# Re-ordering the openings of two deformable-convolution layers: group 0's hats and first dense rows go ahead of bilinear weights, second tap and image 1's sums

## The reference, cut to what matters

```python
off1 = make_offset(conv3x3(x, tm1_w, tm1_b), conv3x3(x, tr1_w, tr1_b))
out = deform_conv(x, off1, dcn1_w)
out = jax.nn.relu(batchnorm(out, bn1_g, bn1_b))
off2 = make_offset(conv3x3(out, tm2_w, tm2_b), conv3x3(out, tr2_w, tr2_b))
out = deform_conv(out, off2, dcn2_w)
out = batchnorm(out, bn2_g, bn2_b)
return jax.nn.relu(out + residual)

# deform_conv: for each pixel and each of 9 taps, 4 corners of x at a
# fractional position, weighed bilinearly; then a product over channels and taps
cols = corner(y0i, x0i, (1 - wy) * (1 - wx)) + corner(y0i, x0i + 1, (1 - wy) * wx) \
     + corner(y0i + 1, x0i, wy * (1 - wx)) + corner(y0i + 1, x0i + 1, wy * wx)
return jnp.einsum('nckhw,ock->nohw', cols, w.reshape(Co, C, K))
```

## Time and profile before

| | us |
|---|---|
| median of 3 runs | 776.32 |
| lowest, highest | 775.11, 782.59 |
| the profiled execution | 783.84 |
| its span, first to last instruction | 782.0 |

### The profile page before, as it was taken

How to read it: one execution, slowest core, us unless ns; L and a number is a source line. 1 busy time by engine, 2 the same in 40 slices (tenths; PEclk the granted TensorE clock), 3 DMA queues, 4 the chain that set the end, 5 groups by cost and what they waited for, 6 DMA issues and landing times.

```text
span 782.0 us, 12373 instructions
## 1 busy us (share of the span) xinstructions
PE 738.1 (94%) x3497; PEld 457.3 (58%) x3497; DVE 598.9 (77%) x1605; ACT 509.3 (65%) x1269; POOL 461.6 (59%) x458
## 2 busy tenths in 40 slices
PE   7889999999999999968999999989998999899997
PEld 6646656555555554654666555545554544678786
DVE  5498879798888879359887998868886878767542
ACT  1756766777777776447776777767776856664342
POOL 3777767777777776067777787777777740000000
PEclk8689999999999999857999999999999999999999
DMA  6969765665766777166886556666777720000001
GB/s 204 312 184 275 244 184 162 195 196 180 207 197 204 207 209 201 55 209 194 246 262 197 174 167 189 182 205 191 207 208 211 208 79 1 1 1 28 1 28 55
DMA packets 55103, 130.13 MB, mean 166 GB/s; under 512 B 8271, under 2 KB 24944, under 8 KB 55036
## 3 DMA queue, kind: packets, MB, share of 16 engines
q0 software_dynamic: 35200, 115.37, 49.4%
q1 hardware_dynamic: 19820, 13.94, 5.7%
q10 hardware_dynamic: 16, 0.03, 0.0%
HBM read 118.76 MB, written 10.55 MB: 165 GB/s over the span
## 4 chain that ended last, share of the span: by engine, by line
PE 76%; DVE 10%; DMA 5%; ACT 4%; issue 3%; POOL 1%; SPq 0%; DVEq 0%; POOLq 0%; ACTq 0%
PE pair L1338 26%; PE pair L1353 10%; PE bank L1497 5%; PE bank L1287 5%; DMA G<-table,rowi 5%; PE bank L1289 4%; PE pair L1322 4%; PE pair L1345 3%; PE pair L1457 2%; PE pair L1432 2%; PE bank L1322 2%; PE pair L1304 2%; PE pair L1479 2%; PE pair L1152 2%; DVE U L928 2%
## 5 line engine op out<-in xcount | busy, mean ns | idle before, releaser
L542 POOL DMA_INDIRECT G<-table,rowi x440 | 453.6, 1031 | 174.0 <-issue 93.9
L1338 PE MATMUL pair<-ST,XT 128*128 128x512 f32 x544 | 261.6, 613 | 7.7 <-ACT CTD L661 7.7
L624 ACT ACTIVATE V<-G,wgt 128x128 f32<-128x128 f32 x440 | 175.1, 398 | 39.1 <-DMA G<-table,rowi 38.4
L626 ACT ACTIVATE U<-G,wgt 128x128 f32<-128x128 f32 x440 | 171.6, 390 | 0.0
L1338 PEld LDWEIGHTS pair<-ST,XT 128*128 128x128 f32 x544 | 105.6, 196 | 109.9 <-issue 83.5
L928 DVE SCALAR_TENSOR_TENSOR V<-G,wgt,V 128x128 f32<-128x128 f32 x440 | 152.5, 347 | 3.7 <-ACT U L626 3.6
L978 DVE TENSOR_TENSOR ST<-pair,stacks 128x512 f32<-128x512 f32 x180 | 119.0, 685 | 45.3 <-PE pair L1322 29.4
L928 DVE SCALAR_TENSOR_TENSOR U<-G,wgt,U 128x128 f32<-128x128 f32 x440 | 152.7, 347 | 0.0
L691 ACT COPY CT<-bank 128x512 f32<-128x512 f32 x110 | 64.3, 585 | 79.2 <-PE bank L1289 70.0
L1353 PE MATMUL pair<-CT,dcn_T 128*128 128x512 f32 x220 | 112.2, 593 | 0.0
L1287 PE MATMUL bank<-band,V 128*128 128x128 f32 x440 | 99.4, 276 | 0.0
(11 more groups left out here) (173 smaller groups left out, 757.3 us busy)
## 6 DMA issues: line engine op xcount, KB each, us to landing
table<-XT SPq DMA_DIRECT2D x16, 512.0 KB, 5.2
G<-table,rowi POOLq DMA_INDIRECT x440, 3.7
out_dram<-G SPq DMA_DIRECT2D x8, 256.0 KB, 2.0
X<-in_x_dram SPq DMA_DIRECT2D x3, 512.0 KB, 6.7
A<-in_L_conv_dcn_w_dram SPq DMA_DIRECT2D x2, 576.0 KB, 8.4
X<-in_x_dram SPq DMA_DIRECT2D x2, 256.0 KB, 2.8
table<-zeros SPq DMA_DIRECT2D x4, 16.0 KB, 2.0
qkv_nat<-in_L_conv_wv_dram SPq DMA_DIRECT2D x1, 64.0 KB
```

What stands on the lines that cost most here:

```text
L542: pool.indirect_dma_start(G[:, i % UNITS, r, :], None, table(n).rearrange("r (e k) -> r e k", e=2), bass.IndirectOffsetOnAxis(rowi[:, at:a ...
L624: act.activation(V[:, i % V_RING, r, :], G[:, i % UNITS, r, 0:C], ACT.Copy, scale=wgt[:, tile:tile + 1, 0])
L626: act.activation(U[:, i % V_RING, r, :], G[:, i % UNITS, r, 3 * C:4 * C], ACT.Copy, scale=wgt[:, tile:tile + 1, 3]).then_inc(scaled[l], 1)
L1338: last = pe.matmul(dense_acc, XT[:, g // IGROUPS * TS + t, :], ST[:, all_y % ST_RING, :], start=(t == 0), stop=(t == QT - 1))
```

## The change

Only order changes, with one bank of accumulators and two row counts. No operation is added or taken away.

- **ROWS.** Group 0's dense rows are used 3, 3, 2 a tap (was 2, 3, 3 and 3, 3, 2).
- **DVE.** `bilinear_weights(0)` is cut in three and interleaved with the hats of group 0, which now start first; `xt_copy(1)` goes behind both. The products of step 0's rows go ahead of `corner_sums(0)` and `offsets(1)`. Positions and row numbers of image 1 go from ahead of the main loop to the end of step 1.
- **PE.** `sum_x(1)` and `sum_y(1)` go between the steps of tap 0's hats; the first three rows are spread ahead of `sum_y(1)`, the second tap and the three setups; `turn(0)` goes behind step 0's dense rows.
- **ACT.** `hats_middle(0)` and `hats_copy(0, 0)` go ahead, and the scalings of blocks 0 and 1 are cut in halves between the copies.
- **PSUM.** Image 1's products go to `conv_acc`, so that `turn_hats(0, 0)` no longer waits for image 1's `z_copy`.

```diff
-        ROWS = [[2, 3, 3, 3, 3, 2], SLOW, QUICK, ...]
+        ROWS = [QUICK, SLOW, QUICK, ...]
@@
-            return (hat_acc if n < AHEAD else job_acc)[:, 0:TS * TAPS * NOFF]
+            return (hat_acc, conv_acc, job_acc)[min(n, AHEAD)][:, 0:TS * TAPS * NOFF]
@@ ACT
                 hats_top(0)
+                hats_middle(0)
                 z_copy(1)
-                hats_middle(0)
+                hats_copy(0, 0)
+                act.wait_ge(wgt_ready, l * N + 1)
+                scale(0, range(0, GTILES // 2))
                 u_copy(1)
-                act.wait_ge(wgt_ready, l * N + 1)
-                scale(0, range(GTILES))
-                hats_copy(0, 0)
+                column_copy(0, 0)
+                scale(0, range(GTILES // 2, GTILES))
                 if l == 0:
                     setup(1)
-                column_copy(0, 0)
+                hats_copy(0, 1)
                 if l == 0:
                     setup(2)
-                hats_copy(0, 1)
+                scale(1, range(0, GTILES // 2))
+                column_copy(0, 1)
                 if l == 0:
                     setup(3)
-                column_copy(0, 1)
-                scale(1, range(GTILES))
+                scale(1, range(GTILES // 2, GTILES))
                 scale(2, range(GTILES))
@@ DVE
-                bilinear_weights(0)
-                xt_copy(1)
@@
                 hats_first(0)
+                corner_distances(0)
                 hats_split(0)
+                corner_hats()
                 hats_last(0)
+                corner_products(0)
+                xt_copy(1)
+                for now in USED[0]:
+                    product(*now)
                 dve.wait_ge(wgt_ready, l * N + 1)
                 corner_sums(0)
                 offsets(1)
-                for now in USED[0]:
-                    product(*now)
                 corner_sums(1)
                 add_halves(1)
                 hats_first(1)
-                dve.wait_ge(off_ready, l * N + AHEAD)
-                positions(1, AHEAD)
-                sample_rows(1, AHEAD)
@@ DVE, end of step i
+                    if i == POSITIONS_NEXT:
+                        dve.wait_ge(off_ready, l * N + AHEAD)
+                        positions(1, AHEAD)
+                        sample_rows(1, AHEAD)
@@ PE
                     products(n, 1)
-                    sum_x(n)
-                    sum_y(n)
+                    if n == 0:
+                        sum_x(n)
+                        sum_y(n)
@@
                 turn_hats(0, 0)
-                if l == 0:
-                    setup(1)
+                sum_x(1)
                 spread_columns(0, 0)
-                if l == 0:
-                    setup(2)
-                turn_hats(0, 1)
-                if l == 0:
-                    setup(3)
-                spread_columns(0, 1)
-                turn(0)
                 pe.wait_ge(xt_dve, l * N + AHEAD)
                 pe.wait_ge(xt_act, l * N + AHEAD)
                 for now in USED[0]:
                     spread_rows(*now)
+                sum_y(1)
+                if l == 0:
+                    setup(1)
+                turn_hats(0, 1)
+                if l == 0:
+                    setup(2)
+                spread_columns(0, 1)
+                if l == 0:
+                    setup(3)
                 for now in USED[1]:
                     spread_rows(*now)
@@ PE, main loop, behind use_dense
+                    if i == 0:
+                        turn(0)
```

More of the change, by code:

```diff
@@ L283, in deform_resblock_attention @@
         RELU = {at - 2: n for n, at in TURN_AT.items()}
+        POSITIONS_NEXT = 1
         POSITIONS = max(SUM_Y) + 1
@@ L291, in deform_resblock_attention @@
         SLOW, QUICK = [2, 2, 2, 2, 3, 3, 2], [3, 3, 2, 3, 3, 2]
-        ROWS = [[2, 3, 3, 3, 3, 2], SLOW, QUICK, QUICK, QUICK, [3, 3, 2] * DENSE[5], SLOW, QUICK]
+        ROWS = [QUICK, SLOW, QUICK, QUICK, QUICK, [3, 3, 2] * DENSE[5], SLOW, QUICK]
         BEGIN = [FIRST[g] - (g > 0) for g in range(GROUPS)]
@@ L876, in sample_rows, with corner_distances @@
                 step(dve.tensor_scalar(low[:, 1, tiles], low[:, 1, tiles], ROUND + W - 2, -ROUND, ALU.min, ALU.add))
-            def bilinear_weights(n):
+            def corner_distances(n):
                 tiles = tile_range(n, n + 1)
@@ L883, in bilinear_weights, with corner_hats @@
                 step(dve.tensor_scalar(dist[:, 1], dist[:, 0], -1.0, None, ALU.add))
+            def corner_hats():
                 for e in range(2):
@@ L889, in bilinear_weights, with corner_products @@
                 step(last)
+            def corner_products(n):
+                tiles = tile_range(n, n + 1)
                 for s, (dy, dx) in enumerate(CORNERS):
@@ L892, in bilinear_weights @@
                 last.then_inc(wgt_ready, 1)
+            def bilinear_weights(n):
+                corner_distances(n)
+                corner_hats()
+                corner_products(n)
             for l in range(LAYERS):
@@ L1299, in turn_hats @@
                     else:
-                        pe.wait_ge(z_act, l * N + AHEAD)
+                        pe.wait_ge(z_act, l * N + 1)
                     to = hat_acc.bitcast(bf16)[0:HK, :].rearrange("q (a t p) -> q a t p", a=2, t=GTILES)
```

## The result

The changed kernel takes 774.75 us (median, 770.02 to 782.38) beside 778.57 us (775.11 to 782.88) for the kernel before in the same series: a ratio of 0.9946, with a 95% interval of 0.9927 to 0.9964. The one run of 782.38 us was a slow one and stands outside that ratio. The ratio is 4.2 us of 776.32 (3.8 by the medians), within 1%: 772.1 us on the scale on which 768.5 was forecast. The range held it; the forecast promised nearly twice the gain.

A forecast was written before the change was run, and what follows sets the result against it. PE was taken to set the pace until the ring fills, then gathers bound both layers' ends. Ring waiting of 8.7 us less 0.7 for PE's clock gave 8 us off 776.3: 768.3, said as 768.5, range 760 to 777.

The forecast's parts named there:

- What bounds the kernel: PE sets the pace until the four-buffer ring is full; POOL's queue is nearly full; both layers end gather-bound behind block 20.
- How a lead reaches the end: At blocks 18 to 20, PE's lead only removes POOL's ring waits: 3.6 us first layer, 1.35 second.
- the middle of 4.95 and 12.5: Ring waiting in the median run, both layers: between 4.95 and 12.5 us, taken as 8.7 us of gain.
- The lower bound: Ring waits at blocks 18 to 20, both layers, all taken away: 4.95 us gained if nothing else moves.
- the clock's 0.7: Deduction of 0.7 us from the 8.7 us gain, for PE's clock, the second rival.
- The lead in the opening: First layer's opening: hats turned at about 21.7 us, first product about 26, first dense rows about 33.5.
- A lead of 7 and 6.5 us: PE's lead in first and second layer; step 3's dense rows at 49 to 51 us in the first.
- The difference between profile and median: Profiled run 7.5 us over the median: if stretched gathers, the median run waits at the ring instead, up to 12.5 us.
- The signs: Timeline checks: first gathers unmoved, no idle over 0.5 us at blocks 17 to 20, block 20 at 117 to 121 us.
- The ring starves: Rival, 6%: late corner_sums(0) delays block 4's gathers and POOL's stream; slower, 784 us and more.
- The clock: Rival, 12%: PE waits longer for late gathers and falls to half clock, 1.8 us once more; 770.3 to 775 us.
- Stretched gathers eat the gain: Rival, 20%: moved DVE work stretches gathers, 1.4 us a hit; six more hits take away 8 us: 776.

The follow-up runs named there:

- the slowest of the others: Changed kernel with positions and row numbers of image 1 put back ahead of the main loop: 781.40 us beside 784.95 for the kernel before, ratio 0.9950.
- the pairs above: Kernel before and changed kernel compared, also with equal edits: gains by medians 3.5 us with five buffers, 3.4 with thin sums, 17.4 with three gathers a block.

## Why the prediction was right or wrong

**What bounds the kernel: half wrong.** PE sets the pace and POOL's queue is nearly full: both right. "Both layers end gather-bound" was wrong for the first layer, where PE takes 234.6 us from block 6 to the last with three gathers or four. In the profile that I had read it took 2.3 us more (236.9), with 1.8 us of waits of PE for `CTD`, and 5.0 more in the slowest of the others (239.6); that is a loss of some executions and not the layer's bound. I had followed the chain back to a gather's landing at 299.13 us and made a bound of a late gather in one execution: in the changed kernel the chain leaves the gathers at 46.93 us for the rest of that layer. Chain of waits, changed kernel (answers the earlier trace rows), two gathers that follow each other in it, and the last:

```profile
46.93 3.80 DMA G<-table,rowi
...
342.16 3.72 DMA G<-table,rowi
...
607.21 3.81 DMA G<-table,rowi
```

For the second layer the step holds: 229.6 us without gathers in the way, 234.0 to 238.6 with them in three profiles of the changed kernel.

**How a lead reaches the end: the step that failed.** "It can only take away the waiting of POOL at blocks 18 to 20" is wrong in both directions. Ring waits are what POOL does while PE sets the pace; taking them away by a fifth buffer is worth 1.5 us (-0.4 to 3.3). A lead reaches the end through PE itself, us for us in the first layer where PE waits for nothing behind block 6. The sum that I built on ring waits, the middle of 4.95 and 12.5, had no ground: in the second profile of before, 8 us shorter than the first, ring waits were 2.4 us, not more than 4.95. The lower bound less the clock's 0.7, 4.95 - 0.7 = 4.25 us, lies beside the measured 4.2 by chance, since it counts another thing.

**The lead in the opening: right at first.** Hats turned at 22.46 us (about 21.7 forecast), first product at 26.89 (26), first dense rows at 33.75 (33.5). In the second layer, counted from the first gather, first dense rows came 19.87 - 11.73 = 8.1 us earlier (4.7 forecast), and step 3's 39.85 - 35.05 = 4.8 (6.5 forecast).

**A lead of 7 and 6.5 us: the mis-sized term.** It measured 1.9 and 3.3 us at block 6. Step 3 was forecast for 49 to 51 us and came at 51.97, at half clock, which I had expected to be cured. I had asked whether `corner_sums(0)` would be too late for the gathers of block 4 (they are not: 28.69 against 37.5 us), and never whether the gathers of blocks 4 and 5 would be there for engines that come earlier. Between the products of blocks 1 and 2 the changed kernel takes 10.1 us, with three gathers a block 6.5, which is 3.6 of the 6.2 us by which its block 6 comes later; the half clock at step 3 is 1.8 of them. With that obstacle gone step 3 stands at 48.70, and the lead is 9.5 and 8.1 us: more than the 7 and 6.5 that I had taken, so the working of the opening itself was not too bold.

**The difference between profile and median: half right.** I took 7.5 us for long gathers. The second and third profiles of before differ from the first by 8.2 and 4.6 us in time, and by 7.4 and 4.1 in long gathers. That they would turn into ring waits was wrong.

**The signs.** First gather unmoved: right in the first layer (15.97, 17.10 and 15.62 in three profiles; 15.62, 17.11 and 17.12 before), wrong in the second, whose first gather follows the first layer's end (327.76, 329.39 and 327.22; 334.80, 330.04 and 331.88 before). No idle time at blocks 17 to 20: right in the first and third profile, wrong in the second, where block 20 itself waits at 122.81: by my own words a sign against the prediction. Longer waits of PE for `CTD` late in the layers did not come: behind block 6 of the second layer they sum to 5.0, 6.0 and 3.1 us in three profiles, 5.9, 3.2 and 4.1 before (those over 0.3 us). Block 20 at 117 to 121: 121.82, 122.81 and 121.3, missed. It was a bad sign, too, since it follows the pace of PE and the luck of long gathers.

**The rivals.** *The ring starves* did not happen. *The clock* did, in another place: at step 3 of the first layer six matmuls took 4.54 us for 2.74, 1.8 us that PE, setting the pace, does not get back. But the kernel before lost as much at step 1 in two of three profiles (4.78 and 4.59 us, 2.74 in the second), and the mean granted clock of the profiled executions is higher in the changed kernel, 0.969, 0.968 and 0.972 of full speed beside 0.957, 0.954 and 0.956: on balance the clock took nothing back. *Stretched gathers eat the gain*: the changed kernel has fewer, not more (29.4, 26.1 and 26.9 us in three profiles, 38.0, 30.7 and 33.9 before), which the medians' gain does not follow (see the pairs above). The rule of the Trainium skill that I had set beside it ("SBUF — State Buffer", section "SBUF: two separate sides": the loser of DVE's and GpSimd's shared port fully blocks; for a DVE instruction with two SBUF inputs the page says so only against a GpSimd instruction that reads SBUF, a condition that I had left out) fits one row better than its neighbour: the gather at 124.38 took 2.34 us, with sums of L938 running from 123.72 on, and the one at 120.39, beside sums that ran from 119.82 to 122.0, took 1.13, only 0.18 over the median.

**What stays open.** Why the gain by medians is 1 to 3 us below the lead at block 6 in some pairs: the second layer gives part of it back to late gathers (in three profiles of the changed kernel it took 237.6, 238.6 and 234.0 us from block 6 on, before 240.1, 236.4 and 238.1), which these few profiles can't size. And nothing was run that would give the opening its gathers earlier; what the lead would bring with all four gathers is therefore known only from the kernels that leave one out, in which no wait of PE over 0.3 us is left behind block 6 either.

## What to carry to other kernels

A lead is worth what is alive of it at the first place where its engines meet a stream that has not moved: here three steps later, at gathers that nothing in the change brings forward. So ask of everything that the earlier work consumes whether it comes earlier too. And to find which stream sets the pace of a stretch, measure the stretch between two of its own instructions in kernels that relieve one stream; a full queue and a late gather in one trace don't tell.

## What the runs showed of the hardware

The time of a gather of 128 rows varies: 942 to 2,940 ns; over the usual 0.946 us each that is 38.0, 30.7 and 33.9 us in three executions of the kernel before, and the time less this sum was 745.8, 744.9 and 745.4 us. In the changed kernel it was 741.6, 748.3 and 741.9 us, so the rule is not a general one. With corner sums cut to 16 channels the sum fell to 12.9 us. PE's share of busy time told nothing throughout: 94% with all gathers, 95% and 96% with three (730.0 us busy in a span of 769.6, 725.0 in 752.5), though late in the second layer gathers set the pace in the former and PE in the latter.
